# A recommendation tower on one core: a turned scratch layout, ids issued earlier, a layer moved behind the grams, and one more looked-up field in the last block

## The reference

```python
combined = jnp.concatenate([dense_features[:, None, :], sparse_features], axis=1)   # (2048, 27, 128)
interactions = jnp.einsum('bfd,bgd->bfg', combined, combined)
iu, ju = jnp.triu_indices(F, k=1)
z = jnp.concatenate([dense_features, interactions[:, iu, ju]], axis=1)
h = jnp.concatenate([z, r_dense_features], axis=1)
h = jnp.maximum(h @ W_top1 + b_top1, 0.0)    # 607 -> 512
h = jnp.maximum(h @ W_top2 + b_top2, 0.0)    # 512 -> 256
y = h @ W_top3                               # 256 -> 1
```

## Time and profile before

| | before |
|---|---|
| median of three runs | 359.31 us (359.15 to 359.65) |
| the profiled execution | 359.83 us, of which 358.0 us are the span |
| granted TensorE clock, mean | 0.986 |
| TensorE busy | 325.9 us (91%), 4192 products |
| VectorE busy | 240.7 us (67%) |
| ScalarE busy | 183.7 us (51%) |
| GpSimd busy | 250.0 us (70%), 256 indirect DMAs |
| DMA packets | 48,069, 44.80 MB; 26,790 of them under 512 B |

### The profile page before, as it was taken

One profiled execution on the slowest core, in us unless ns is written; L12 is line 12 of the kernel. 1 busy time (PEld: TensorE's weight loads), 2 busy tenths in 40 slices (PEclk: granted clock), 3 DMA queues, 4 the chain that ended last, 5 costly groups with the idle time before them and its releaser, 6 DMA issues.

```text
span 358.0 us, 10391 instructions
## 1 busy us (share of the span) xinstructions
PE 325.9 (91%) x4192; PEld 312.3 (87%) x4192; DVE 240.7 (67%) x721; ACT 183.7 (51%) x360; POOL 250.0 (70%) x264
## 2 busy tenths in 40 slices
PE   0558789999999999999999999999999999999576
PEld 0548679989999998999899999999899999998565
DVE  3889987996469762995389654986299556951012
ACT  1345555556633763457534664557445664366224
POOL 5777777777777777777777777777777777775020
PEclk9987999999999999999999999999999999999989
DMA  5999657664447434662457444653356344421230
GB/s 146 235 249 246 157 160 193 158 168 133 99 101 181 115 76 103 139 170 69 99 120 187 95 82 106 149 149 69 103 131 185 82 98 102 125 68 46 34 78 0
DMA packets 48069, 44.80 MB, mean 125 GB/s; under 512 B 26790, under 2 KB 42150, under 8 KB 48022
## 3 DMA queue, kind: packets, MB, share of 16 engines
q1 hardware_dynamic: 38448, 26.89, 31.8%
q0 software_dynamic: 8320, 16.87, 19.5%
q10 hardware_dynamic: 1254, 0.39, 0.6%
HBM read 39.33 MB, written 4.78 MB: 123 GB/s over the span
## 4 chain that ended last, share of the span: by engine, by line
PE 81%; DVE 7%; DMA 6%; SPq 2%; ACT 2%; issue 1%; POOL 0%; ACTq 0%
PE ps_o L335 39%; PE ps_m L386 16%; PE ps_g L375 15%; PE ps_t L346 7%; DVE onehot L749 5%; DMA oh_ids<-onehot_ids 3%; DVE tbl_lo L734 2%; DMA interaction_scratch<-inter 2%; PE ps_m L416 2%; SPq L207 1%; DMA x<-interaction_scratch 1%; PE ps_g L446 1%; POOL interaction_scratch L190 0%; SPq L228 0%; ACT emb L555 0%
## 5 line engine op out<-in xcount | busy, mean ns | idle before, releaser
L313 POOL DMA_INDIRECT rows<-tables,idx x256 | 247.4, 966 | 80.4 <-issue 76.9
L749 DVE TENSOR_SCALAR onehot<-oh_ids,rownum 125x256 fp32r<-125x256 int32 x640 | 200.2, 388 | 50.9 <-PE ps_o L335 43.1
L335 PE MATMUL ps_o<-onehot,tbl_hi 125*128 125x256 f32 x640 | 163.9, 295 | 22.0 <-DVE tbl_lo L734 21.8
L335 PE MATMUL ps_o<-onehot,tbl_lo 125*128 125x256 f32 x640 | 159.0, 287 | 0.0
L335 PEld LDWEIGHTS ps_o<-onehot,tbl_hi 125*128 125x128 f32 x640 | 125.0, 195 | 27.3 <-DVE tbl_lo L734 23.3
L335 PEld LDWEIGHTS ps_o<-onehot,tbl_lo 125*128 125x128 f32 x640 | 125.4, 196 | 0.0
L555 ACT ACTIVATE emb<-ps_o 128x256 f32<-128x256 f32 x80 | 49.3, 740 | 87.0 <-PE ps_o L335 87.0
L375 PEld LDWEIGHTS ps_g<-emb 128*54 128x54 f32 x2048 | 53.6, 130 | 4.8 <-issue 1.8
L375 PE MATMUL ps_g<-emb 128*54 128x54 f32 x2048 | 56.0, 214 | 1.8 <-ACT emb L581 0.8
L571 ACT ACTIVATE emb<-ps_t 128x512 f32<-128x512 f32 x63 | 45.8, 729 | 9.9 <-PE ps_t L346 9.6
L595 ACT ACTIVATE inter<-ps_g 128x432 f32<-128x432 f32 x64 | 33.9, 532 | 15.6 <-PE ps_g L375 13.1
(11 more groups left out here) (60 smaller groups left out, 206.5 us busy)
## 6 DMA issues: line engine op xcount, KB each, us to landing
oh_ids<-onehot_ids SPq DMA_DIRECT2D x80, 128.0 KB
rows<-tables,idx POOLq DMA_INDIRECT x256, 2.4
x<-interaction_scratch SPq DMA_DIRECT2D x23, 117.0 KB
inter<-small_tables SPq DMA_DIRECT2D x4, 448.0 KB
interaction_scratch<-inter SPq DMA_DIRECT2D x30, 47.2 KB
x<-small_tables SPq DMA_DIRECT2D x3, 448.0 KB
h<-small_tables SPq DMA_DIRECT2D x3, 448.0 KB
interaction_scratch<-inter SPq DMA_DIRECT2D x32, 38.2 KB
```

The lines of the kernel that those rows point to most:

```text
L313: pool.indirect_dma_start(rows[e][:, k, :], None, tables[k], bass.IndirectOffsetOnAxis(ap=idx[:, NG * hh + k:NG * hh + k + 1], axis=0),).t ...
L335: mm = pe.matmul(o, tbl[p][:, k, c, :], onehot[n % SLOTS_OH][:, c, :], start=(c + p == 0), stop=(c == TCHUNKS - 1 and p == 1))
L749: op = nc.vector.tensor_scalar(onehot[n % SLOTS_OH][:, c, :], oh_ids[0:TPART, n % IDS, :], rownum[:, c:c + 1], None, ALU.is_equal)
```

## The change

Five edits. `scratch` now has q as its first axis, so a store's run is a feature's whole row (8 to 21 times 256 B), and a chunk of x is loaded by four DMAs, one for each q, with runs of 256 B. Two of the first id loads stand earlier in SyncE's queue. In the last block TensorE computes `layer2(6, 0)` after `grams(15)` instead of ahead of it. Field 25, moved to the end of `GATHER`, is not gathered in the last block but looked up as an eleventh field: its table is loaded to `h` by one DMA of 125 partitions, behind the x loads of block 6, and split on ScalarE (amid the placing of the lookups) and VectorE into the place of `tbl[0]`, the table of field 3. The last block's stores and loads are divided anew over the queues of SyncE, ScalarE and GpSimd, whose wait is gone.

```diff
-GATHER = [f for f in range(FIELDS) if f not in ONEHOT]
+EXTRA = 25
+GATHER = [f for f in range(FIELDS) if f not in (*ONEHOT, EXTRA)] + [EXTRA]
+    def group(hh, g):
+        s, n = GROUPS[g]
+        return s, n - (hh // 2 == BLOCKS - 1 and g == NGR - 1)
-    scratch = nc.dram_tensor("interaction_scratch", (FEATURES, WRAP, QUAD, TB), f32,
+    scratch = nc.dram_tensor("interaction_scratch", (QUAD, FEATURES, WRAP, TB), f32,
...
-                eng.dma_start(scratch[f0:f1, f0 + 1:g1, q, :],
+                eng.dma_start(scratch[q, f0:f1, f0 + 1:g1, :],
...
-        def load_x(eng, i, c):
+        def load_x(eng, i, c, quads):
...
-            eng.dma_start(x[0:PAIR_ROWS, c, :], src).then_inc(x_loaded[c], 16)
+            for q in quads:
+                src = bass.AP(tensor=scratch.tensor, offset=((q * FEATURES + PAIR_F * c) * WRAP + PAIR_F * c + 1) * TB,
+                              ap=[[TB, SHIFTS], [(WRAP + 1) * TB, PAIR_F], [1, TB]])
+                eng.dma_start(x[0:PAIR_ROWS, c, TB * q:TB * (q + 1)], src).then_inc(x_loaded[c], 16)
...
+            def load_extra():
+                sp.wait_ge(l3_done, LAST - 1)
+                sp.dma_start(extra_stage, extra_table).then_inc(extra_loaded, 16)
...
             load_ids(1)
+            load_ids(2)
             load_stage(sp, 1)
-            load_ids(2)
+            load_ids(3)
...
             load_stage(sp, 3)
-            load_ids(3)
...
+                else:
+                    load_extra()
+                    load_ids(NO * BLOCKS)
...
-            store_band(sp, LAST, 0, range(0, 2), inter_stored[0])
-            store_band(sp, LAST, 1, range(QUAD), inter_stored[1])
+            for b in range(2):
+                store_band(sp, LAST, b, range(0, 2), inter_stored[b])
+            store_wrapped(sp, LAST, range(0, 2))
+            load_x(sp, LAST, 0, range(0, 2))
             for c in range(1, PAIR_CHUNKS):
-                load_x(sp, LAST, c)
+                load_x(sp, LAST, c, range(QUAD))
...
-            pool.wait_ge(inter_stored[0], 16 * QUAD * BLOCKS)
             store_band(pool, LAST, 2, range(QUAD), last_stored)
...
+                if k == NO:
+                    pe.wait_ge(extra_split, 1)
...
                 lookups(LAST)
+                lookup(LAST, NO)
...
                 transposes(b, 2)
-                layer2(m, 0)
                 last_transposes()
                 grams(b)
+                layer2(m, 0)
                 layer2(m, 1)
...
             def relu1(m, n, src):
+                if (m, n) == (LAST - 1, 0):
+                    act.wait_ge(extra_split, 1)
...
+                    if i == LAST and u == 2:
+                        act.wait_ge(extra_loaded, 16)
+                        act.wait_ge(onehot_used, 2 * (NO * LAST + 1))
+                        nc.scalar.activation(extra_parts[0], extra_stage, ACT.Copy).then_inc(extra_hi, 1)
                     if u == NGR - 1:
                         split_x_hi(i - 1, X_ORDER)
+                if i == LAST:
+                    place_onehot(i, NU)
...
-                store_band(act, LAST, 0, range(2, QUAD), inter_stored[0])
-                store_wrapped(act, LAST, range(QUAD))
+                for b in range(2):
+                    store_band(act, LAST, b, range(2, QUAD), inter_stored[b])
+                store_wrapped(act, LAST, range(2, QUAD))
                 relus2(m)
-                load_x(act, LAST, 0)
+                load_x(act, LAST, 0, range(2, QUAD))
...
+                if i == LAST:
+                    dve.wait_ge(extra_hi, 1)
+                    nc.vector.tensor_tensor(extra_parts[1], extra_stage, extra_parts[0].bitcast(f32), ALU.subtract).then_inc(extra_split, 1)
+                    make_onehot(NO * BLOCKS)
                 split_x_lo(i - 1, range(XCHUNKS))
```

More of the change, by code:

```diff
@@ L29, with build_tower @@
 TB = 2 * QROWS
-def build_tower(nc, dense_t, dense_e, gather_ids, onehot_ids, tables, small_tables, row_numbers,
+def build_tower(nc, dense_t, dense_e, gather_ids, onehot_ids, extra_ids, tables, small_tables, row_numbers,
                 identity, w1_pairs, w1_dense, b1, w2, b2, w3, out):
@@ L120, in build_tower @@
         stage_split = sem("stage_split")
+        extra_loaded = sem("extra_loaded")
+        extra_hi = sem("extra_hi")
+        extra_split = sem("extra_split")
         w1_dense_added = sem("w1_dense_added")
@@ L178, in split_of @@
             return (N1 if n in (NO + 1, DENSE_ITEM) else 1024, *parts)
+        extra_table = small_tables[NO].rearrange("(p c) d -> p (c d)", c=TCHUNKS)
+        extra_stage = stage[1][0:TPART, :]
+        extra_parts = [t[:, 0, :, :].rearrange("p c d -> p (c d)") for t in tbl]
         block = ctx.enter_context(nc.Block())
@@ L248, in turn_interactions @@
                 for c in range(PAIR_CHUNKS):
-                    load_x(sp, i, c)
+                    load_x(sp, i, c, range(QUAD))
             def store_y(m):
@@ L308, in _ @@
                     pool.wait_ge(idx_loaded[hh // 2], 16)
-                for g, (s, n) in enumerate(GROUPS):
+                for g in range(NGR):
+                    s, n = group(hh, g)
                     wait(pool, transposed, NGR * (hh - 2) + g + 1)
@@ L340, in transposes @@
             def transposes(hh, g):
-                e, (s, n) = hh % 2, GROUPS[g]
+                e, (s, n) = hh % 2, group(hh, g)
                 q = NGR * hh + g
-                pe.wait_ge(gathered[e][g], 16 * n * (hh // 2 + 1))
+                pe.wait_ge(gathered[e][g], 16 * (GROUPS[g][1] * (hh // 2) + n))
                 wait(pe, rows_placed, q - 1)
@@ L350, in last_transposes @@
             def last_transposes():
-                e, g, (s, n) = 1, NGR - 1, GROUPS[-1]
+                e, g, (s, n) = 1, NGR - 1, group(HALVES - 1, NGR - 1)
                 q = NGR * HALVES - 1
-                pe.wait_ge(gathered[e][g], 16 * (n * BLOCKS - 1))
+                pe.wait_ge(gathered[e][g], 16 * (GROUPS[g][1] * LAST + n - 1))
                 pe.wait_ge(rows_placed, q - 1)
@@ L361, in last_transposes @@
                 pe.wait_ge(last_gathered, 16)
-                pe.transpose(ps_m[1][:, 0:128], rows[e][:, NG - 1, :], ident[:, :]).then_inc(last_transposed, 1)
+                pe.transpose(ps_m[1][:, 0:128], rows[e][:, s + n - 1, :], ident[:, :]).then_inc(last_transposed, 1)
             def grams(hh):
@@ L366, in grams @@
                 pe.wait_ge(rows_placed, NGR * (hh + 1))
-                pe.wait_ge(onehot_placed, 2 * NU * (i + 1))
+                pe.wait_ge(onehot_placed, 2 * (NU * (i + 1) + (i == LAST)))
                 pe.wait_ge(dense_placed, hh + 1)
@@ L424, in last_layer1 @@
                         pe.wait_ge(rows_placed, NGR * HALVES)
-                        pe.wait_ge(onehot_placed, 2 * NU * BLOCKS)
+                        pe.wait_ge(onehot_placed, 2 * (NU * BLOCKS + 1))
                     r = PAIR_ROWS if c < PAIR_CHUNKS else 128
@@ L544, in place_onehot @@
             def place_onehot(i, u):
-                n = len(UNITS[u])
+                n = len(UNITS[u]) if u < NU else 1
                 act.wait_ge(onehot_used, 2 * (NO * i + 2 * u + n))
-                f = 1 + NG + 2 * u
+                f = 1 + NG + 2 * u if u < NU else NG
                 for e in range(2):
@@ L566, in place_rows @@
                     wait(act, gram_done, FILLS * (hh - 1))
-                s, n = GROUPS[g]
+                s, n = group(hh, g)
                 q = NGR * hh + g
@@ L574, in place_last_rows @@
             def place_last_rows():
-                s, n = GROUPS[-1]
+                s, n = group(HALVES - 1, NGR - 1)
                 q = NGR * HALVES - 1
@@ L580, in place_last_rows @@
                 act.wait_ge(last_transposed, 1)
[L581 removed]
+                nc.scalar.activation(emb_view(1)[:, :, s + n], ps_m[1][:, 0:128], ACT.Copy).then_inc(rows_placed, 1)
             def copy_grams(hh):
@@ L599, in split_x_hi @@
                     r = 128 if c == PAIR_CHUNKS else PAIR_ROWS
-                    act.wait_ge(x_loaded[c], 16 * (m + 1))
+                    act.wait_ge(x_loaded[c], 16 * (m + 1) * (1 if c == PAIR_CHUNKS else QUAD))
                     if c == PAIR_CHUNKS:
@@ L817 @@
     onehot_ids = ids[..., ONEHOT].transpose(0, 2, 1)
+    extra_ids = ids[BLOCKS - 1, :, EXTRA].reshape(1, BLOCK)
     dense_t = a["r_dense_features"].reshape(BLOCKS, BLOCK, DIM).transpose(0, 2, 1)
@@ L835 @@
         "onehot_ids": onehot_ids.reshape(BLOCKS, 1, len(ONEHOT) * BLOCK),
+        "extra_ids": extra_ids,
         "tables": [a[f"tbl_{f}"] for f in GATHER],
-        "small_tables": [a[f"tbl_{f}"] for f in ONEHOT],
+        "small_tables": [a[f"tbl_{f}"] for f in (*ONEHOT, EXTRA)],
         "row_numbers": np.arange(SMALL_ROWS, dtype=np.float32).reshape(SMALL_ROWS // 8, 8),
```

11 lines of the change are left out of this document (4 added, 7 removed).

## The result

| | before | after |
|---|---|---|
| median | 359.41 us (359.15 to 359.65, 4 runs) | 372.74 us (372.14 to 373.35, 4 runs) |
| the profiled execution, its span | 359.83 us, 358.0 us | 373.35 us, 371.5 us |
| granted TensorE clock, mean | 0.986 | 0.977 |

The change makes the kernel slower by 13.3 us: ratio 1.0376, 95% interval 1.0354 to 1.0398. The forecast was 366.7, range 358.5 to 371.5: the sign holds, and the mechanism up to the last grams; the size does not, and for the tail the mechanism was wrong in part.

A forecast was written before the change was run, and what follows sets the result against it. TensorE was taken to bound the kernel, with VectorE holding it at the start and DRAM traffic at the end. -1.9 + 0.5 + 8.3 + 1.3 - 1.1 + 0.3 = +7.4 gave a 366.7 us median, range 358.5 to 371.5.

The forecast's parts named there:

- The tail: From the last grams' copy (T): stores land sooner, but SyncE's ten loads put chunk 2 at T + 13.0, not 12.8: +0.3 us.
- the eleventh lookup with its clock: Block 7: TensorE waits for the table issued behind twelve loads, +8.3 us, then runs at half clock, +1.3 us.
- the start: Blocks 0 and 1: sooner ids, -1.9 us, and chunk 2 of x late for TensorE, +0.5 us.
- layer 2: Last block: 1.43 us of products move behind the grams, which begin 1.1 us earlier: -1.1 us.
- Early ids: Block 0: VectorE no longer waits for the fourth ids but somewhat for the fifth: -1.9 us (gain 0 to 2.7).
- x in block 1: Block 0's turn: twelve load issues make chunk 2 late for TensorE's layer 1: +0.5 us (0 to 0.8).
- the stores play no part: Before block 7: stores, done at 302.6, do not delay the table; the ids wait for VectorE until 303.3.
- The first: Rival on x loads: 256 B runs issue as quickly as a store, 0.36 us; 354.8 us in all, chance 0.17.
- The second: Rival on block 7: the table lands in 4.5 us like a cut one, clock holds; 363.2 us, chance 0.15.
- the third: Rival on x loads: 1.1 us each, chunk 2 late in every block, table at 324; about 372 us, chance 0.06.

The follow-up runs named there:

- plain rows: The changed kernel with each x load reading 117 plain rows of 256 B from the small tables instead of 13 x 9 from scratch: 360.76 us, 1.0034.
- the ids between: The changed kernel with field 25's table cut at partition 112 and ahead of the x loads, its ids between chunk 0's and chunk 1's loads: 364.98 us, 1.0144.
- the old layout, cut and ahead: The changed kernel with the earlier scratch layout, one load per chunk, field 25's table cut at partition 112 and ahead of the x loads: 358.65 us, 0.9988.
- the table ahead: The changed kernel with field 25's uncut table issued ahead of the twelve x loads instead of behind them: 367.43 us, 1.0181.

## Why the prediction was right in direction and short in size

The trace is 6.1 us longer than the step by step sum had it. The tail is short by 3.8, the eleventh lookup with its clock by 2.2, the start by 0.4, and layer 2 gave 0.2 more.

**Early ids, -1.9 and +0.5 for x in block 1: measured -1.0.** The wait for the fourth ids went, as the step says, and the fifth were not waited for either, so VectorE won more than the step's best case. What failed is the sentence that the gain stays, "since VectorE sets the pace to the end of block 0 and TensorE from there". The gathers take part of it back in blocks 0 and 6 (with early ids alone in blocks 4 to 6). They are visible before: 32 gathers of 1.25 us to a block of 39.4. How much they take differs from one execution to the next: in the kernels with early ids block 7 begins between 295.73 and 297.90, against 297.06 before, so the -1.0 is that of one trace, and early ids alone gained nothing that the runs can tell. Chunk 2 of block 1 was late as predicted; TensorE waited 1.4 us for it.

**The eleventh lookup with its clock, +8.3 and +1.3: measured +11.8.** The order of events was right at every step: 0.77 us for a load, the table issued at 314.1 (forecast 314.0), ScalarE's wait, TensorE's idle time of 8.4 and then half clock (3.50 us for 16 products, 1.6 more than at full). Short were the twelve loads (10.9 for 10.2) and the landing (7.7 for 6.7). And the block began 1.0 us sooner, which the table could not follow entirely, since the sixteen stores, 7.0 us of issue instead of 6, ended just ahead of the ids (302.73 and 302.77): "the stores play no part" was wrong, if only by half a microsecond.

**Layer 2, -1.1: measured -1.3**, and -1.0 by itself.

**The tail, +0.3: measured +4.1.** This is the largest mistake, and two terms of the step failed. First, I let SyncE issue its ten loads in a row from T + 2.6, and priced only bands 0 and 2. Chunks 1 and 2 wait for the wrapped stores too (chunk 0 for its band alone), and these stand last in both queues. They were in at T + 7.0, so eight loads, not ten, had to be issued behind that: 7.0 + 7 x 0.82 + 2.2 is T + 15.0. In the old layout (the kernel with ids, layer 2 and division) the same stores, last issued at T + 3.9, are in at T + 7.0 too: with this division of the stores the long runs bought nothing. With the old division the stores that chunk 1 waits for were in sooner by them, at T + 5.6 with the layout alone and T + 7.4 before. Second, the clock: the step says that TensorE may lose some there, and put no number on it, where the stretch behind the last split came out 1.9 us longer. In all six kernels with four loads to a chunk of this form the clock was at half for 10.2 us or more, and the rest took 10.4 to 12.1 us behind the last split. The kernels with four loads to a chunk differ from the others in the spacing of their splits as well, so how the 1.9 us divide between the clock and the spacing stays open.

**The rivals.** The first, a quick load, was false for this form of load. Its condition could be made true with plain rows, and then it gave 360.8 and not 354.8: the table takes 7.0 us to land and TensorE waits for it, and in the tail x's last split came at T + 11.6, where the rival had it land at T + 8.7. The second, a table that lands in 4.5 us, was false for 125 partitions and true for the cut one (4.6); but the clock did not hold, and the cut table alone brought the kernel to 1.030 and not to 363.2. In the third, loads of 1.1 us, the time is near the measured one for a wrong reason: they took 0.77. What I left out of the range is a tail in which stores land late and the clock falls as well.

The loss divides, by the ratios, in three: 8.3 us for an uncut table and its ids behind twelve loads (after against the ids between), 5.6 for the layout when only x stands behind the loads, all of it behind T (the ids between against the old layout, cut and ahead), and -0.4 for the rest, which is not clear of zero. Why the clock stays low for 10.2 us in one tail and 3.4 in another was not tried by itself. In the six tails with 10.2 or more the last split stands 3.2 us or more behind the one before it, in all others 2.6 at most; but with splits 2.0 and then 2.5 or 0.9 us apart the clock was at half for 3.4 us in some and 6.8 in others, so the gap doesn't explain it all.

## What to carry to other kernels

Before a store is made cheaper at the price of more loads, count the issues on the queue that carries both, with the duration of that form of access, and list all that stands behind them: here it is a table and its ids, for which TensorE waits. A transfer that several stores release begins when the last of them lands, so each of its semaphores needs a time of its own. And a gain at the start of a kernel is worth only the distance to the next engine's pace: 4 us for VectorE moved the start of block 7 by 1.3 us at best, with the gathers 0.6 us a block slower than TensorE, and the kernel's time by nothing that could be told.

## What the runs showed of the hardware

- The issue of a load from 13 by 9 rows onto 117 partitions took SyncE 0.77 us with runs of 256 B and 0.79 with 1 KB; from 117 plain rows of 256 B it took 0.38 (median of 94 each; 23 in the kernel before).
- With the new division of the last stores, nine and thirteen rows of 3.3 to 5.4 KB landed no sooner than the same bytes in runs of 256 B: the last of the wrapped stores was in at T + 7.0 with either layout, though the long ones were issued within 3.3 us and the short ones in 4.6. Over the traces it was T + 6.6 to 7.0 with the long rows and T + 6.9 to 7.1 with the short runs. The last long one took 4.4 us from its issue, the last short one 3.1. With the old division, in which GpSimd's stores wait, the long ones that chunk 1 waits for were in at T + 5.6, 3.1 us from the last wrapped one's issue, and the short ones at T + 7.4. Whether GpSimd's stores, issued from T + 0.3 on in the new division, are what slows the long ones was not tried by itself.
- Half a megabyte in 125 partitions took 7.7 us from its issue to its use in the kernel after, 8.9 with the table ahead, 7.0 with plain rows and 10.0 with the old layout; cut at partition 112 it took 4.6. The Trainium skill (DMA: Bandwidth & Descriptors, "Why a DMA increments its semaphore by 16 and not by 1") has the number of engines as the largest up to 16 that divides the slowest dimension of both sides. That is 5 for 125 and 16 for 112, and the times of these runs agree.
- TensorE's clock stood at 1.2 GHz for 6.8 us after 8.4 us idle ahead of the eleventh lookup, and for 3.4, 6.8, 10.2 or 13.7 us in the tails.
